# Moving the staging of the down-projection weights to the GpSimd queue and one group later, in an eight-core attention and FFN layer

## The chip, the cores and the metric

The kernel runs as one program on all 8 cores of a Trainium2 chip, with no traffic between the cores. The metric is the device time of the slowest core in microseconds. Each core handles half the tokens of one of four batch items, and holds its own copy of every weight.

## The reference

Everything is float32 with shapes x (4, 2048, 2048), 16 heads of 128, and an FFN width of 8192:

```python
def reference(x, w_atten, w_proj, w_gate, w_up, w_down):
    xn = layernorm(x)                                   # over the last axis, no affine
    q, k, v = split(xn @ w_atten.T)                     # 16 heads of 128
    q, k = rope(q), rope(k)
    att = softmax(causal(q @ k.T / sqrt(128)))
    s = (att @ v) @ w_proj.T
    h = silu(xn @ w_gate) * (xn @ w_up)
    h = keep_2_largest_of_4(h)                          # by magnitude, along the width
    g = silu(h @ w_down)
    return x + s * g
```

## The kernel before

A small recorder (`emit`, `dma`) notes for each of five engines a list of instructions, each with its waits on semaphores; `finalize` plays each list back in the order in which it was recorded. So an engine executes strictly in program order, and an instruction that waits holds back everything recorded behind it on the same engine. SP and POOL (GpSimd) issue the DMAs, each its own in that order. All buffers come from one SBUF arena that is reused by stages.

The stages on each core:

1. *Layernorm* (0 to about 185 us): x of all 2048 tokens of the batch item is loaded, normalized and kept in SBUF as bf16 (`xn`). `xn_done` are its four last instructions.
2. *Attention* (185 to 2115 us): a loop over 8 groups of two heads. For each group, the weights wk, wv and wq (2 MB of f32 each) are loaded by SP into the staging buffer `wstag2` and cast to bf16 by VectorE (L348). Then TensorE computes the K and Q units (12 of 16 matmuls each, L368); ScalarE evicts each unit (L381), a swap matmul (L390) and three VectorE operations (L393, L396, L404) apply RoPE. Two PSUM banks and two bf16 buffers rotate through the units, and the RoPE of a unit is recorded behind the matmuls of the next. V follows (L422), then scores, exp and PV for four pairs of head and query block (L457 to L492), each ended by a reciprocal (L504), a product on VectorE (L513) and a store of y from POOL. The weight casts wait for the last use of the bf16 weights by the group before.
3. *Out-projection* (from 2118 us): y is loaded back, w_proj is loaded and cast, `s` is stored to DRAM.
4. *Gate and up projections* (2325 to 3500 us) with the 2-of-4 selection, the result stored transposed as `d_hT`.
5. *Down-projection* (from 3505 us), which reads bf16 weights from the DRAM tensor `d_wdb`.

`d_wdb` is filled during stage 2: w_down (`wd`, 64 MB of f32) is loaded in pieces, cast by VectorE (L332) and spilled to `d_wdb` (32 MB of bf16) by POOL. Before the change this happens at the head of each group, ahead of that group's wk, wv and wq: 8 pieces of 1 MB for each of the 8 groups, in rows of 512 B (128 columns of f32), issued by SP into two f32 buffers and cast into two bf16 buffers. The load of piece s waits for the cast of piece s-2, and the cast of piece s for the spill of piece s-2. The loads of y and w_proj that open stage 3 wait for the last two spills.

`wstag2` has one buffer, so each of the three weight loads of a group waits for the cast of the one before it:

```python
            sl = 0
            t_l = kb.dma("sync", wstag2[sl][:].rearrange("p (c d) -> p c d", d=256),
                         srcw, sem,
                         [stag_free.get(sl)] + (xn_done if g == 0 else []))
            t_c = E("vector", lambda e, wbf=wbf, sl=sl: e.tensor_copy(
                wbf[:], wstag2[sl][:]), [t_l, wfree[nm]], "DVE")
            stag_free[sl] = t_c
```

Of the kernel before, what the change touches and what calls it, by code (L numbers as in the profile page):

```python
# [9 lines left out]
BF16 = mybir.dt.bfloat16  # L10
# [4 lines left out]
NF = C // 128  # L15
NT = T // 512
OWN = T // 2
NG = 8
# [96 lines left out]
def build_nc():  # L115
# [8 lines left out]
    wd = nc.dram_tensor("wd", [I, C], F32, kind="ExternalInput").ap()  # L124
# [10 lines left out]
    d_wdb = nc.dram_tensor("d_wdb", [128, NIC * C], BF16).ap()  # L135
# [11 lines left out]
    A = Arena(arena_t.ap(), ARENA_COLS)  # L147
# [18 lines left out]
    kb = KB(nc)  # L166
    E = kb.emit
# [38 lines left out]
    xn_done = []  # L206
# [75 lines left out]
        dbg_xn_tok = kb.dma("gpsimd", dbg["xn"][:], xn[:], "dbg0", xn_done)  # L282

    A.mark()
    wstag2 = [A.alloc(NF * 256)]
    wq_bf = A.alloc(NF * 128, BF16)
    wk_bf = A.alloc(NF * 128, BF16)
    wv_bf = A.alloc(NF * 128, BF16)
# [8 lines left out]
    recip = A.alloc(512)  # L297
    rep_sb = A.alloc(512)
    y_sb = A.alloc(256, BF16)
    wdp_st2 = [A.alloc(16 * 128) for _ in range(2)]  # L300
    wdp_bf2 = [A.alloc(16 * 64, BF16) for _ in range(2)]

    wqv = wq_bf[:].rearrange("p (c d) -> p c d", d=256)
    wkv = wk_bf[:].rearrange("p (c d) -> p c d", d=256)
# [14 lines left out]

    wdp_cast = {}  # L320
    wdp_spill = {}
    for g in range(NG):
        for j in range(8):
            s_ = g * 8 + j
            fcw, qi = s_ // 4, s_ % 4
            sl2 = s_ % 2
            srcw = wd[qi * 2048:(qi + 1) * 2048, fcw * 128:(fcw + 1) * 128]\
                .rearrange("(c p) d -> p c d", p=128)
            t_wpl = kb.dma("sync", wdp_st2[sl2][:].rearrange("p (c d) -> p c d", d=128),
                           srcw, "dWQ0" if sl2 == 0 else "dWQ1",  # L330
                           [wdp_cast.get(s_ - 2)] + (xn_done if s_ == 0 else []))
            t_wpc = E("vector", lambda e, sl2=sl2: e.tensor_copy(  # L332
                wdp_bf2[sl2][:], wdp_st2[sl2][:]),
                [t_wpl, wdp_spill.get(s_ - 2)], "DVE")
            wdp_cast[s_] = t_wpc
            t_wps = kb.dma("gpsimd", d_wdb[:, s_ * 2048:(s_ + 1) * 2048],
                           wdp_bf2[sl2][:], "dWDS0" if sl2 == 0 else "dWDS1", [t_wpc])
            wdp_spill[s_] = t_wps
        toks_w = {}
        for wi, (wap, wbf, nm, sem) in enumerate(  # L340
                ((wkT, wk_bf, "k", "dW0"), (wvT, wv_bf, "v", "dW1"),
                 (wqT, wq_bf, "q", "dW2"))):
            srcw = wap[:, g * 256:(g + 1) * 256].rearrange("(c p) d -> p c d", p=128)
            sl = 0
            t_l = kb.dma("sync", wstag2[sl][:].rearrange("p (c d) -> p c d", d=256),
                         srcw, sem,
                         [stag_free.get(sl)] + (xn_done if g == 0 else []))
# [3 lines that stand above are left out]
            toks_w[nm] = t_c  # L351
# [170 lines left out]
        kv_read_tok = group_pe_tail  # L522
        wfree = {"q": q_last_mm, "k": k_last_mm, "v": v_last_mm}

    ph2_tail_pe = kv_read_tok
    ph2_tail_dve = prev_y
    ph2_tail_act = prev_rpe
# [5 lines left out]
    wp_bf = [A.alloc(NF * 256, BF16) for _ in range(2)]  # L533
    s_stage = A.alloc(512)
    yav = y_all[:].rearrange("p (c x) -> p c x", x=OWN)
    wdp_last = [wdp_spill[62], wdp_spill[63]]
    t_yb = kb.dma("sync", yav, d_y[:, :].rearrange("(c p) x -> p c x", p=128), "dYB",
                  y_spills + wdp_last + [ph2_tail_pe, ph2_tail_dve, ph2_tail_act,
                                         stag_free.get(0), stag_free.get(1)])
# [392 lines left out]
```

How the kernel before makes its waits and increments, by code:

```python
                def body(handle):  # L76
                    for waits, fn, inc in ops:
                        for s, v in waits:
                            handle.wait_ge(sems[s], v)
                        ins = fn(handle)
                        if inc is not None:
                            s, by = inc
                            ins.then_inc(sems[s], by)
```

## Time and profile before

| | us |
|---|---|
| timed runs, median of 2 | 4029.93 |
| timed runs, lowest and highest | 4005.47, 4054.39 |
| the profiled execution, device time | 4059.74 |
| its span on the slowest core (core 6) | 4058.2 |
| spans of the eight cores | 3944.8 to 4058.2 |

| engine | busy us | share of the span |
|---|---|---|
| TensorE matmul (PE) | 2797.2 | 69% |
| TensorE weight load (PEld) | 1210.0 | 30% |
| VectorE (DVE) | 1329.8 | 33% |
| ScalarE (ACT) | 603.6 | 15% |
| GpSimd (POOL) | 226.5 | 6% |

The profile follows one execution on the slowest core. Busy time is the time in which an engine executes; DMA-issuing instructions are not counted as busy. Idle time is put down to the engine or transfer whose semaphore came last. "SPq" and "POOLq" are the queues that issue DMAs; a DMA's time to landing runs from its issue to the arrival of its semaphore. The granted clock of TensorE is given as a share of 2.4 GHz; 0.5 is the lower of its two levels. Buffer numbers are left out of the names, and as everything lies in one arena, most SBUF tiles read as `arena`.

### The profile page before, as it was taken

How to read it: one execution, taken by the hardware profiler on the slowest of the kernel's cores; microseconds unless marked ns; L12 is line 12 of the kernel's file. 1: busy time of each engine (PE TensorE's matmuls, PEld its weight loads, DVE VectorE, ACT ScalarE, POOL GpSimd, SP SyncE). 2: the span in 40 equal slices, each digit the busy share in tenths (PEclk: the TensorE clock that was granted, in tenths of full speed). 3: DMA queues.
4: the chain of work that ended last, by engine and by line, in shares of the span. 5: the costliest groups of instructions: out<-in, count | busy, mean ns of one | idle time of the engine just before them, and what ended most of it. 6: DMA issues, size and time to landing. Idle time of an engine off the chain costs nothing.

```text
span 4058.2 us, 34754 instructions; the slowest of 8 cores (3944.8 to 4058.2 us)
## 1 busy us (share of the span) xinstructions
PE 2797.2 (69%) x12377; PEld 1210.0 (30%) x12592; DVE 1329.8 (33%) x2087; ACT 603.6 (15%) x1102; POOL 226.5 (6%) x356
## 2 busy tenths in 40 slices
PE   2248385683838558383865769898889889399598
PEld 0013141321404123140411234343334334144244
DVE  4631131313213131221311046656657466300000
ACT  1102112030211203021120111111111111000000
POOL 0000000000000000000000100100001000011011
PEclk7668687886969778696887989999999999799799
DMA  4260512406041140604116176555465664455664
GB/s 150 84 171 3 149 42 67 124 4 188 3 137 53 53 139 4 188 2 121 49 34 207 69 158 156 122 142 135 104 146 131 135 141 99 144 177 210 198 209 155
DMA packets 513481, 466.99 MB, mean 115 GB/s; under 512 B 10144, under 2 KB 468896, under 8 KB 508832
## 3 DMA queue, kind: packets, MB, share of 16 engines
q1 hardware_dynamic: 486176, 376.65, 34.6%
q0 software_dynamic: 27136, 88.10, 6.5%
q8 instruction: 104, 1.70, 0.2%
q14 instruction: 65, 0.53, 0.0%
HBM read 393.41 MB, written 71.30 MB: 115 GB/s over the span
## 4 chain that ended last, share of the span: by engine, by line
PE 51%; DMA 23%; DVE 14%; issue 6%; SPq 3%; ACT 2%; DVEq 0%; ACTq 0%; POOLq 0%
PE ps L810 11%; PE ps L723 11%; PE ps L368 6%; PE ps L422 6%; DMA arena<-wd 5%; DMA d_hT<-arena 4%; DMA arena<-wkT 4%; PE ps L469 4%; PE ps L486 3%; SPq L66 3%; PE ps L457 3%; DVE arena L504 3%; PE ps L492 3%; PE ps L565 2%; DMA arena<-wqT 2%
## 5 line engine op out<-in xcount | busy, mean ns | idle before, releaser
L723 PE MATMUL ps<-arena 128*128 128x512 bf16 x4005 | 955.4, 394 | 34.1 <-DVE arena L699 27.6
L368 PE MATMUL ps<-arena 128*128 128x512 bf16 x1504 | 369.9, 400 | 472.8 <-DVE arena L348 468.6
L723 PEld LDWEIGHTS ps<-arena 128*128 128x128 bf16 x4096 | 412.2, 102 | 524.8 <-issue 90.6
L810 PE MATMUL ps<-arena 128*128 128x512 bf16 x2007 | 451.8, 384 | 95.8 <-issue 49.0
L368 PEld LDWEIGHTS ps<-arena 128*128 128x128 bf16 x1536 | 155.7, 102 | 683.9 <-issue 522.1
L504 DVE RECIPROCAL arena<-ps 1x512 f32<-1x512 f32 x32 | 107.1, 3346 | 757.2 <-PE ps L486 757.2
L810 PEld LDWEIGHTS ps<-arena 128*128 128x128 bf16 x2048 | 206.8, 101 | 340.5 <-issue 99.2
L473 ACT ACTIVATE arena<-ps 128x512 bf16<-128x512 f32 x384 | 229.3, 597 | 315.8 <-PE ps L469 306.4
L422 PE MATMUL ps<-arena 128*128 128x256 bf16 x2048 | 231.7, 274 | 0.0
L422 PEld LDWEIGHTS ps<-arena 128*128 128x128 bf16 x2048 | 203.4, 99 | 27.7
L735 DVE TENSOR_TENSOR arena<-arena,ps 128x256 f32<-128x256 f32 x256 | 105.3, 417 | 297.9 <-ACT arena L732 297.6
L699 DVE CAST arena<-arena 128x2048 bf16<-128x2048 f32 x128 | 157.2, 1228 | 135.9 <-DMA arena<-wgu 127.2
L732 ACT ACTIVATE arena<-ps 128x256 f32<-128x256 f32 x256 | 98.1, 384 | 690.4 <-PE ps L723 625.6
L469 PE MATMUL ps<-arena 128*128 128x512 bf16 x376 | 153.3, 408 | 64.1 <-PE ps L422 9.3
L381 ACT CAST arena<-ps 128x512 bf16<-128x512 f32 x96 | 56.3, 586 | 891.2 <-PE ps L368 751.1
L833 DVE TENSOR_TENSOR arena<-arena 128x512 f32<-128x512 f32 x32 | 22.2, 694 | 497.0 <-ACT arena L821 497.0
L565 PE MATMUL ps<-arena 128*128 128x512 bf16 x501 | 123.6, 398 | 87.6 <-ACT arena L572 47.5
L332 DVE CAST arena<-arena 128x2048 bf16<-128x2048 f32 x64 | 77.9, 1227 | 282.0 <-DMA arena<-wd 211.7
L457 PE MATMUL ps<-arena 128*128 128x512 bf16 x376 | 163.0, 433 | 6.8 <-PE ps L457 4.2
L664 PE MATMUL ps<-arena 128*128 128x128 bf16 x512 | 52.4, 228 | 157.3 <-DVE arena L647 154.3
L486 PE MATMUL ps<-arena 128*1 128x512 bf16 x384 | 152.9, 398 | 7.5 <-ACT arena L473 6.7
L66 POOL DMA_DIRECT2D d_hT<-arena x128 | 97.5, 762 | 1078.9 <-DVE arena L735 799.9
(71 smaller groups left out, 1841.6 us busy)
## 6 DMA issues: line engine op xcount, KB each, us to landing
arena<-wgu SPq DMA_DIRECT2D x128, 1024.0 KB, 15.5
arena<-wd SPq DMA_DIRECT2D x64, 1024.0 KB, 12.4
arena<-d_wdb SPq DMA_DIRECT2D x32, 2048.0 KB, 8.6
d_wdb<-arena POOLq DMA_DIRECT2D x64, 512.0 KB, 8.9
arena<-xT SPq DMA_DIRECT2D x4, 4096.0 KB, 16.1
arena<-wkT SPq DMA_DIRECT2D x8, 2048.0 KB, 20.6
arena<-wvT SPq DMA_DIRECT2D x8, 2048.0 KB, 8.3
arena<-wqT SPq DMA_DIRECT2D x8, 2048.0 KB, 9.4
```

The lines of the kernel that those rows point to most:

```text
L66: return self.emit(eng, lambda e: e.dma_start(out=out, in_=in_), waits, inc=sem, inc_by=16)
L368: tok = E("tensor", lambda e, f=f, h2=h2, bank=bank, tile=tile, wv_=wv_: e.matmul(ps[bank][:], wv_[:, f, h2 * 128:(h2 + 1) * 128], xnv[:, ...
L422: tok = E("tensor", lambda e, f=f, tc=tc, bank=bank: e.matmul(ps[bank][:, 0:256], xnv[:, f, tc * 128:(tc + 1) * 128], wvv[:, f, :], start= ...
L457: t_s = E("tensor", lambda e, qpos=qpos, h2=h2, a=a, sbank=sbank: e.matmul(ps[[0, 1, 4][sbank]][:], kh[:, h2 * T + qpos * 128:h2 * T + (qp ...
L469: t_mm = E("tensor", lambda e, mi=mi, sbank=sbank: e.matmul(ps[[0, 1, 4][sbank]][:], id_sb[:], mk_sb[:, mi * 512:(mi + 1) * 512], start=Fa ...
L473: t_e = E("scalar", lambda e, sbank=sbank, slot=slot: e.activation(pT[slot][:], ps[[0, 1, 4][sbank]][:], AF.Exp, bias=EXP_BIAS, scale=EXP_ ...
L486: last=(qi == nL - 1): e.matmul(ps[3][0:1, :], ones_colb[:, 0:1], pT[slot][:], start=first, stop=last),
L504: t_rcp = E("vector", lambda e: e.reciprocal(recip[0:1, :], ps[3][0:1, :]), [den_last, prev_rpe], "DVE")
L565: wpv=wpv: e.matmul(ps[bank][:], wpv[:, yc, cc * 128:(cc + 1) * 128], yav[:, yc, tt2 * 512:(tt2 + 1) * 512], start=(yc == 0), stop=(yc == ...
L699: t_gc = E("vector", lambda e, ip=ip, qt=qt, qs=qs: e.tensor_copy(wgu_bf[ip % 2][:].rearrange("p (c d) -> p c d", d=512) [:, :, qt * 128:( ...
L723: tok = E("tensor", lambda e, f=f, tc=tc, bank=bank, gv=gv: e.matmul(ps[bank][:], xnv[:, f, tc * 128:(tc + 1) * 128], gv[:, f, :], start=( ...
L810: tok = E("tensor", lambda e, ic=ic, bank=bank, wdv=wdv: e.matmul(ps[bank][:], wdv[:, ic, :], hTv[:, ic, :], start=(ic == 0), stop=(ic == ...
```

## The change

The staging of `wd` is put into a function `wdp_prep(g)`. It handles 16 pieces of 512 KB for a group instead of 8 of 1 MB, with one f32 and one bf16 buffer instead of two of each, and issues the loads from POOL instead of SP. The load of a piece waits for the cast of the piece before, and the cast for the spill of the piece before. It is recorded at the head of group g for group g-1, so group 0 begins without it, and once more after the last group for group 7. `wstag2` gets two buffers that alternate over the stream of weight loads. Stage 3 waits for the last two of the now 128 spills.

```diff
-    wstag2 = [A.alloc(NF * 256)]
+    wstag2 = [A.alloc(NF * 256) for _ in range(2)]
...
-    wdp_st2 = [A.alloc(16 * 128) for _ in range(2)]
-    wdp_bf2 = [A.alloc(16 * 64, BF16) for _ in range(2)]
+    wdp_st2 = [A.alloc(8 * 128)]
+    wdp_bf2 = [A.alloc(8 * 64, BF16)]
...
+    def wdp_prep(g):
+        for j in range(16):
+            s_ = g * 16 + j
+            fcw, qi = s_ // 8, s_ % 8
+            srcw = wd[qi * 1024:(qi + 1) * 1024, fcw * 128:(fcw + 1) * 128]\
+                .rearrange("(c p) d -> p c d", p=128)
+            t_wpl = kb.dma("gpsimd", wdp_st2[0][:].rearrange("p (c d) -> p c d", d=128),
+                           srcw, "dWQ0" if s_ % 2 == 0 else "dWQ1",
+                           [wdp_cast.get(s_ - 1)] + (xn_done if s_ == 0 else []))
+            t_wpc = E("vector", lambda e: e.tensor_copy(wdp_bf2[0][:], wdp_st2[0][:]),
+                      [t_wpl, wdp_spill.get(s_ - 1)], "DVE")
+            wdp_cast[s_] = t_wpc
+            t_wps = kb.dma("gpsimd", d_wdb[:, s_ * 1024:(s_ + 1) * 1024],
+                           wdp_bf2[0][:], "dWDS0" if s_ % 2 == 0 else "dWDS1", [t_wpc])
+            wdp_spill[s_] = t_wps
+
     for g in range(NG):
-        for j in range(8):
-            s_ = g * 8 + j
-            fcw, qi = s_ // 4, s_ % 4
-            sl2 = s_ % 2
-            srcw = wd[qi * 2048:(qi + 1) * 2048, fcw * 128:(fcw + 1) * 128]\
-                .rearrange("(c p) d -> p c d", p=128)
-            t_wpl = kb.dma("sync", wdp_st2[sl2][:].rearrange("p (c d) -> p c d", d=128),
-                           srcw, "dWQ0" if sl2 == 0 else "dWQ1",
-                           [wdp_cast.get(s_ - 2)] + (xn_done if s_ == 0 else []))
-            t_wpc = E("vector", lambda e, sl2=sl2: e.tensor_copy(
-                wdp_bf2[sl2][:], wdp_st2[sl2][:]),
-                [t_wpl, wdp_spill.get(s_ - 2)], "DVE")
-            wdp_cast[s_] = t_wpc
-            t_wps = kb.dma("gpsimd", d_wdb[:, s_ * 2048:(s_ + 1) * 2048],
-                           wdp_bf2[sl2][:], "dWDS0" if sl2 == 0 else "dWDS1", [t_wpc])
-            wdp_spill[s_] = t_wps
+        if g > 0:
+            wdp_prep(g - 1)
...
-            sl = 0
+            sl = (3 * g + wi) % 2
...
+    wdp_prep(NG - 1)
     ph2_tail_pe = kv_read_tok
...
-    wdp_last = [wdp_spill[62], wdp_spill[63]]
+    wdp_last = [wdp_spill[126], wdp_spill[127]]
```

## Rows read from the trace of the kernel before

**Rows 1.** Waits: engine line waited for: us in total, times, longest.
```profile
PE ps L368 <- DVE arena L348: 468.6, 8, 80.4
```

**Rows 2.** One stretch: PE, PEld, DVE, ACT, POOL busy, clock, DMA share, GB/s.
```profile
680.00:735.00 55.00, 0.00 (x0) 0.00 (x0) 12.16 (x10) 0.00 (x0) 5.19 (x9) 0.50 0.79 231
```

**Rows 3.** VectorE's timeline there: start us, us, instruction, idle before.
```profile
679.90 0.69 DVE L513 TENSOR_TENSOR arena<-ps,arena 128x512 bf16<-128x512 f32 x1 [3.16 <-ACT arena L510]
680.51 2.36 DVE L332 CAST arena<-arena 128x2048 bf16<-128x2048 f32 x2
...
724.90 1.23 DVE L332 CAST arena<-arena 128x2048 bf16<-128x2048 f32 x1 [4.71 <-DMA arena<-wd]
733.08 2.29 DVE L348 CAST arena<-arena 128x4096 bf16<-128x4096 f32 x1 [6.95 <-DMA arena<-wkT]
744.30 2.29 DVE L348 CAST arena<-arena 128x4096 bf16<-128x4096 f32 x1 [8.93 <-DMA arena<-wvT]
756.17 2.29 DVE L348 CAST arena<-arena 128x4096 bf16<-128x4096 f32 x1 [9.57 <-DMA arena<-wqT]
758.38 0.68 DVE L393 TENSOR_TENSOR arena<-arena 128x512 f32<-128x512 bf16 x1
```

**Rows 4.** Timeline of the SP queue, same stretch.
```profile
711.52 7.18 SPq L66 DMA_DIRECT2D arena<-wkT  x1
735.46 0.37 SPq L66 DMA_DIRECT2D arena<-wvT  x1
746.70 0.37 SPq L66 DMA_DIRECT2D arena<-wqT  x1
```

**Rows 5.** Timeline of ScalarE, same stretch: evictions of the K units.
```profile
741.63 0.59 ACT L381 CAST arena<-ps 128x512 bf16<-128x512 f32 x1 [61.97 <-PE ps L368]
745.09 0.59 ACT L381 CAST arena<-ps 128x512 bf16<-128x512 f32 x1 [2.87 <-PE ps L368]
759.15 0.59 ACT L381 CAST arena<-ps 128x512 bf16<-128x512 f32 x1 [13.48 <-DVE arena L393]
765.95 0.59 ACT L381 CAST arena<-ps 128x512 bf16<-128x512 f32 x1 [6.20 <-PE ps L368]
769.62 0.59 ACT L381 CAST arena<-ps 128x512 bf16<-128x512 f32 x1 [3.09 <-PE ps L368]
```

**Rows 6.** Timeline of POOL, same stretch.
```profile
681.13 0.72 POOL L66 DMA_DIRECT2D d_y<-arena  x1 [29.41 <-DVE arena L513]
682.27 0.73 POOL L66 DMA_DIRECT2D d_wdb<-arena  x1 [0.42 <-issue]
...
695.09 0.53 POOL L66 DMA_DIRECT2D d_wdb<-arena  x1 [11.14 <-DVE arena L332]
```

**Rows 7.** DMA issues: count, KB each, median us to landing.
```profile
arena<-wd SPq DMA_DIRECT2D x64, 1024.0 KB, 12.4
...
d_wdb<-arena POOLq DMA_DIRECT2D x64, 512.0 KB, 8.9
...
arena<-wvT SPq DMA_DIRECT2D x8, 2048.0 KB, 8.3
...
d_hT<-arena POOLq DMA_DIRECT2D x128, 128.0 KB, 3.1
...
d_s<-arena POOLq DMA_DIRECT2D x32, 256.0 KB, 2.6
...
d_y<-arena POOLq DMA_DIRECT2D x32, 128.0 KB, 2.0
```

**Rows 8.** The transfers of wd, whole span.
```profile
DMA to landing us min/median/max: 7.0/12.4/14.6
```

**Rows 9.** Group 0: SP's first wd issue, and ScalarE's eviction of K unit 3.
```profile
185.66 37.33 SPq L66 DMA_DIRECT2D arena<-wd  x8
...
281.49 0.59 ACT L381 CAST arena<-ps 128x512 bf16<-128x512 f32 x1 [5.97 <-PE ps L368]
```

**Rows 10.** SP's first issue of the out-projection stage.
```profile
2118.05 0.37 SPq L66 DMA_DIRECT2D arena<-d_y  x1
```

## The prediction, made before the result was known

> **What bounds the kernel now.** I read the page first. TensorE is busy for most of the span but idles in eight long holes, all in the attention stage between 185 and 2115 us. The table of waits puts 468.6 us of that idle time on one pair: the K matmuls of L368 wait for the weight cast of L348, eight times, 80.4 us at the longest [rows 1]. The question is what sits ahead of that weight cast, and for this I read one hole engine by engine, the one between groups 1 and 2.
>
> The stretch table shows the hole itself: from 680 to 735 us TensorE executes nothing, its clock is at the lower of its two levels (0.50 of 2.4 GHz), and the 16 DMA engines are 79% busy at 231 GB/s [rows 2]. VectorE's timeline shows why [rows 3]. The last attention output of the group (L513) ends at 680.59. Behind it in VectorE's program stand eight wd casts; they end at 726.13, most of them waiting for a load or a spill. Only then come the casts of wk (733.08), wv (744.30) and wq (756.17), each late by a transfer, because there is one staging buffer. RoPE starts at 758.38. SP's timeline gives the other side: wk is issued at 711.52, after the last wd load; wv at 735.46 and wq at 746.70, each behind the cast that frees the buffer [rows 4].
>
> What follows the hole is read from ScalarE's evictions [rows 5]. K unit 0 is evicted at 741.63, 6.3 us after the wk cast ends (735.37; the unit starts on the slow clock), unit 1 at 745.09, 3.46 us later. Then TensorE's swap matmul for the second RoPE waits for VectorE's first RoPE, which stands behind the wq cast, and unit 2's eviction waits 13.48 us. Unit 3 is evicted at 765.95; from there TensorE runs undisturbed. So one boundary costs 765.95 - 680.59 = 85.4 us, which I round to 85 and use for all seven boundaries between groups.
>
> **The change part by part.** Three things change: who issues the wd loads, how the wd work is cut and buffered, and how many staging buffers the QKV weights have.
>
> *VectorE's order does not change in kind.* The wd casts of group g-1 are now emitted at the head of group g, still ahead of the wk, wv and wq casts. VectorE executes in program order, so the weight casts still wait for the whole wd block, as in [rows 3]. The block of group 0 goes; a block after the last group comes. There remain eight blocks on the critical path, of 8 MB each.
>
> *The block becomes a serial chain.* It is now 16 steps with one f32 and one bf16 buffer. The load of step s+1 waits for cast s; cast s+1 waits for that load and for spill s. Nothing is loaded ahead, since the POOL queue holds the first load of a block behind the last y spill, and before two loads were always in flight or landed: the first two casts run back to back at 680.51. One step, s:
> - from VectorE's end to POOL's start 0.54 us (680.59 to 681.13). On POOL the spill stands ahead of the next load: 0.53 us to issue (695.09), then 0.42 us to the next instruction (681.13 + 0.72 to 682.27) [rows 6]. That is 1.5 us together.
> - the load from issue to landing, L.
> - 0.1 us to the cast (wq: issued 746.70, cast at 756.17 for a transfer of 9.4) and 0.7 us for the cast: 1.23 us for 2048 columns and 2.29 for 4096 [rows 3] make 0.16 + 0.52 per 1000, so 0.69 for 1024.
> - the spill, of 256 KB like POOL's stores of d_s (2.6 us, [rows 7]), is issued 0.95 us before the load and should land before it, so it adds nothing unless L is under about 2.
> So s = 2.3 + L.
>
> *L has no row.* No POOL load of 512 KB in 1024 runs of 512 B is in the trace. Four ways to bound it, from [rows 7]. Far below: POOL's 128 KB store of y lands in 2.0 us. Below: the quickest 1024 KB wd load from SP lands in 7.0 us [rows 8], and half of it is 3.5. Between: take 1.4 us fixed (2.0 less 128 KB at 231 GB/s) and the step's load and spill, 768 KB together, at the 231 GB/s of the hole, 3.4 us: 4.8. Above: 2.0 for y, 1.7 for 384 KB more at that rate, and a price for each run: d_hT (128 KB in 512 runs) takes 3.1 us against 2.0 for 128 runs, so 896 more runs add 2.6 us: 6.3. The last counts some of the cost of short runs twice. I take 5.0, near the middle value, and keep 3.5 to 6.3. Then s = 7.3 and a block is 117 us where 45.5 us stand now.
>
> The Trainium skill, DMA: Bandwidth & Descriptors, section on the anatomy of a SWDGE DMA, gives a fit of about 2.0 us plus bytes over 436 GB/s; for 512 KB that is an estimate of 3.2 us, so s of 5.5 and a change of +185 us instead of +415. The fit has no term for the length of the runs, while here d_hT and y, of the same bytes, differ by 1.1 us.
>
> *The QKV weights gain.* With SP free of wd and two staging buffers, wk and wv of the next group are loaded during the present one, hundreds of microseconds early. Call T0 the end of the block. The wk cast ends at T0 + 2.4, the wv cast follows at once, and wq is issued when the wk cast frees its buffer, lands 9.4 us later and is cast by about T0 + 14.3; RoPE starts then. By the spacing of [rows 5] (3.46, then 3.67 us) units 0 to 3 are evicted 6.3, 9.7, 13.4 and 17.1 us after the wk cast, and the swap matmul that stalled now finds its RoPE nearly done; I give it 0.3 us. Unit 3 is evicted at T0 + 19.9. Per boundary: 16 s + 20 - 85 = 16 s - 65.
>
> *Group 0.* Nothing stands ahead of wk now. It is issued at 185.66, where the first wd load is [rows 9]; alone a 2 MB load takes 8.3 us [rows 7], with wv behind it I give it 12. wk cast to 200.3, unit 3 evicted at 217.6 instead of 281.49: -64 us.
>
> *The end.* The last block, 16 s, stands wholly between the last y and the out-projection, since the loads of y and wp wait for the last two wd spills; SP issues the former at 2118.05 now [rows 10], about as long after the last y as it will be after the last spill: +16 s.
>
> *What costs nothing.* The same bytes are moved; stages 3 to 5 are untouched. The casts' busy time is about the same, 128 x 0.69 = 88 us against 64 x 1.23 = 79 us, already in s.
>
> **Sum:** 7 (16 s - 65) - 64 + 16 s = 128 s - 519 us. At s = 7.3: +415 us. The profiled execution took 4059.7 us, so 4475; it lies 30 us above the median of the two timed runs, 4029.9, and I forecast against the median: 4445 us. Within 2% (80 us) is what I call no change.
>
> **Rivals.**
> *A. The load lands fast.* L about 3.5, half the quickest wd load, because with one load in flight the DMA engines are unloaded. Then s = 5.8 and +223: 4253 us. For it: the DMA engines will be mostly idle. Against: half of a transfer's time also halves its fixed part. The rule of the skill named above lies here. Chance 0.22.
> *B. POOL's software queue is slow on 1024 short runs.* L = 7.9, between the quickest 1 MB load and the 8.9 us that POOL's 512 KB d_wdb spills take under load [rows 7]: s = 10.2, +787: 4817 us. For it: d_hT against y. Against: those medians come from crowded stretches. It decides from L above about 6.6. Chance 0.18.
> *C. It is not slower.* The weights' prefetch repays the serial chain. The break-even is s = 4.05, L = 1.8 us; up to s = 4.7, L = 2.4 us, the kernel is within 2%. That would need a 512 KB load to land like POOL's y store of 128 KB (2.0 us) or its d_s store of 256 KB (2.6 us); at 2.2 it gives +57: 4087 us. For it: nothing but the empty DMA engines. Chance 0.03.
> *Forecast*, L from 3.8 to 6.6: 0.57.
>
> **How the numbers follow.** The range runs from rival A's price, 4250, to L = 6.5, where 128 x 8.8 - 519 is +607: 4640. It leaves out most of B, C and the lower tail of A, 2 in 10. A, B and the forecast are all slower by over 2%; C holds 0.03 for the same, and I leave 0.01 for faster, an overlap that I do not see.
>
> **What the profile of the changed kernel will show.** Sixteen wd casts of 0.69 us ahead of each wk cast but the first, spaced 7.3 us apart and each waiting for its load; a TensorE hole of about 120 us before each of groups 1 to 7 and one of some 120 us between the last attention output and the out-projection; wk and wv casts back to back behind the block; unit 2's eviction no longer waiting 13 us for RoPE; the first K unit at about 200 us. The prediction is wrong if the spacing is off 7.3 us (each microsecond is 128 us of time), if the spill and not the load ends the wait of the casts, or if the loads of a block start before the last y.

## The result, and the profile after

| | before | after |
|---|---|---|
| median of the timed runs, us | 4053.72 (10 runs) | 4455.64 (13 runs) |
| lowest and highest, us | 4005.47, 4167.24 | 4383.4, 4588.76 |
| ratio after / before | | 1.089, 95% interval 1.083 to 1.095 |
| profiled execution, span of the slowest core, us | 4058.2 | 4422.6 |

The kernel became 8.9% slower. The ratio is made from runs in which no die was held at a lower clock than the other; the medians of the table are over all runs.

The stage borders, read from the SP queue's timeline, say where the time went. The kernel after, columns start us, us, instruction:

```profile
182.07 0.37 SPq L66 DMA_DIRECT2D arena<-wkT  x1
...
2506.86 0.37 SPq L66 DMA_DIRECT2D arena<-d_y  x1
```

Before, the last layernorm instruction ended and the first wd load was issued at 185.66 [rows 9], and the first transfer of the out-projection at 2118.05 [rows 10]: 1932 us of attention. After, 182.07 to 2506.86: 2325 us, so 392 us more. The rest of the span went from 1940 to 1916 us, 24 us less, and layernorm took 4 us less. The whole loss lies in the attention stage. (That is the slowest core of each execution. In the mean of the eight cores the first transfer of the out-projection starts at 2115 and at 2493 us, 378 us later, and the stages behind it are 30 us shorter.)

The waits of the whole span (waiting engine, line, what it waited for: us, times, longest):

```profile
PE ps L371 <- DVE arena L351: 843.1, 8, 116.0
DVE arena L332 <- DMA arena<-wd: 801.3, 128, 7.9
```

L371 is the old L368, L351 the old L348. TensorE's wait for the weight cast went from 468.6 us [rows 1] to 843.1, and every one of the 128 wd casts waits for its own load, never for a spill. VectorE at the boundary between groups 1 and 2:

```profile
663.32 0.69 DVE L516 TENSOR_TENSOR arena<-ps,arena 128x512 bf16<-128x512 f32 x1 [3.16 <-ACT arena L513]
670.02 0.70 DVE L332 CAST arena<-arena 128x1024 bf16<-128x1024 f32 x1 [6.02 <-DMA arena<-wd]
676.79 0.69 DVE L332 CAST arena<-arena 128x1024 bf16<-128x1024 f32 x1 [6.07 <-DMA arena<-wd]
...
774.13 0.69 DVE L332 CAST arena<-arena 128x1024 bf16<-128x1024 f32 x1 [7.41 <-DMA arena<-wd]
774.74 4.50 DVE L351 CAST arena<-arena 128x4096 bf16<-128x4096 f32 x2
788.94 2.29 DVE L351 CAST arena<-arena 128x4096 bf16<-128x4096 f32 x1 [9.70 <-DMA arena<-wqT]
791.15 0.69 DVE L396 TENSOR_TENSOR arena<-arena 128x512 f32<-128x512 bf16 x1
```

The output of the group ends at 664.01, where it ended at 680.59 before [rows 3]. Then the sixteen casts, 6.8 us apart for most, end at 774.82. The casts of wk and wv follow back to back; only wq still waits. POOL's timeline shows one step: cast end 670.72, spill issued at 671.26, next load at 671.80, its cast at 676.79.

```profile
671.26 0.55 POOL L66 DMA_DIRECT2D d_wdb<-arena  x1 [5.28 <-DVE arena L332]
671.80 0.91 POOL L66 DMA_DIRECT2D arena<-wd  x1
```

The DMA issue of the spills (count, KB each, median us to landing), and the landing of the wd loads (min/median/max):

```profile
d_wdb<-arena POOLq DMA_DIRECT2D x128, 256.0 KB, 2.3
```

```profile
DMA to landing us min/median/max: 4.6/4.9/6.3
```

The evictions after the hole, ScalarE, to be held against [rows 5]:

```profile
783.30 0.59 ACT L384 CAST arena<-ps 128x512 bf16<-128x512 f32 x1 [120.22 <-PE ps L371]
...
791.93 0.59 ACT L384 CAST arena<-ps 128x512 bf16<-128x512 f32 x1 [4.58 <-DVE arena L396]
796.57 0.59 ACT L384 CAST arena<-ps 128x512 bf16<-128x512 f32 x1 [4.05 <-PE ps L371]
```

Unit 2 (791.93) waits 4.58 us where it waited 13.48; unit 3 is evicted at 796.57.

### The profile page after: what moved, and what is told of

The parts are those of the page before. It is cut to its first block, busy times and chain, and to the rows that moved or that the text cites. A ratio compares the mean times of both kernels' runs of the same rounds, so it can differ in the third digit from the quotient of the medians.

```text
span 4422.6 us, 35311 instructions; the slowest of 8 cores (4308.5 to 4422.6 us)
## 1 busy us (share of the span) xinstructions
PE 2796.9 (63%) x12592; PEld 1203.5 (27%) x12592; DVE 1340.6 (30%) x2151; ACT 603.5 (14%) x1102; POOL 387.3 (9%) x548
## 4 chain that ended last, share of the span: by engine, by line
PE 46%; DMA 27%; DVE 13%; issue 7%; SPq 2%; ACT 2%; POOL 2%; DVEq 0%; ACTq 0%; POOLq 0%
DMA arena<-wd 14%; PE ps L814 10%; PE ps L727 9%; PE ps L371 6%; PE ps L425 5%; DMA d_hT<-arena 4%; PE ps L472 4%; PE ps L489 3%; PE ps L495 3%; PE ps L460 3%; SPq L66 2%; DVE arena L507 2%; DMA arena<-wgu 2%; DVE arena L332 2%; PE ps L569 2%
## 5 line engine op out<-in xcount | busy, mean ns | idle before, releaser
L727 PE MATMUL ps<-arena 128*128 128x512 bf16 x4096 | 952.1, 391 | 26.9 <-DVE arena L703 26.9
L371 PE MATMUL ps<-arena 128*128 128x512 bf16 x1536 | 363.4, 392 | 843.1 <-DVE arena L351 843.1
L814 PE MATMUL ps<-arena 128*128 128x512 bf16 x2048 | 454.4, 384 | 77.8 <-DMA arena<-d_wdb 77.8
L371 PEld LDWEIGHTS ps<-arena 128*128 128x128 bf16 x1536 | 152.1, 99 | 1046.3 <-issue 875.5
L332 DVE CAST arena<-arena 128x1024 bf16<-128x1024 f32 x128 | 88.9, 695 | 801.3 <-DMA arena<-wd 801.3
L569 PE MATMUL ps<-arena 128*128 128x512 bf16 x512 | 127.1, 405 | 200.6 <-DVE arena L557 151.6
L703 DVE CAST arena<-arena 128x2048 bf16<-128x2048 f32 x128 | 157.2, 1228 | 135.5 <-DMA d_s<-arena 84.8
L472 PE MATMUL ps<-arena 128*128 128x512 bf16 x384 | 159.5, 415 | 57.5 <-PE ps L460 0.4
L460 PE MATMUL ps<-arena 128*128 128x512 bf16 x384 | 168.3, 438 | 4.9 <-ACT arena L434 4.9
L495 PE MATMUL ps<-arena 128*128 128x512 bf16 x384 | 158.8, 414 | 0.0
## 6 DMA issues: line engine op xcount, KB each, us to landing
arena<-wqT SPq DMA_DIRECT2D x8, 2048.0 KB, 10.3
```

The lines of the kernel that those rows point to most:

```text
L371: tok = E("tensor", lambda e, f=f, h2=h2, bank=bank, tile=tile, wv_=wv_: e.matmul(ps[bank][:], wv_[:, f, h2 * 128:(h2 + 1) * 128], xnv[:, ...
L460: t_s = E("tensor", lambda e, qpos=qpos, h2=h2, a=a, sbank=sbank: e.matmul(ps[[0, 1, 4][sbank]][:], kh[:, h2 * T + qpos * 128:h2 * T + (qp ...
L472: t_mm = E("tensor", lambda e, mi=mi, sbank=sbank: e.matmul(ps[[0, 1, 4][sbank]][:], id_sb[:], mk_sb[:, mi * 512:(mi + 1) * 512], start=Fa ...
L495: first=(qi == 0), last=(qi == nL - 1): e.matmul(ps[2][:], vg[:, qpos * 256 + h2 * 128:qpos * 256 + (h2 + 1) * 128], pT[slot][:], start=fi ...
L569: wpv=wpv: e.matmul(ps[bank][:], wpv[:, yc, cc * 128:(cc + 1) * 128], yav[:, yc, tt2 * 512:(tt2 + 1) * 512], start=(yc == 0), stop=(yc == ...
L727: tok = E("tensor", lambda e, f=f, tc=tc, bank=bank, gv=gv: e.matmul(ps[bank][:], xnv[:, f, tc * 128:(tc + 1) * 128], gv[:, f, :], start=( ...
```

## The experiments

The first theory, that of the prediction: eight blocks of wd work lie on the path because VectorE meets them ahead of the weight casts, and a block is long because its pieces form a serial chain. The prediction gave two reasons for the chain, the single buffer and the spill that stands ahead of the next load on POOL; theory 1 below puts it on the second, POOL's program order. Rivals: the single buffer alone, POOL's queue alone, and a part of the block that lies beside other work. The size of the pieces and the delay by one group were not varied by themselves. All ran on all 8 cores; the kernel "before" was timed beside each.

### Two buffers, in the same order

```diff
-    wdp_st2 = [A.alloc(8 * 128)]
-    wdp_bf2 = [A.alloc(8 * 64, BF16)]
+    wdp_st2 = [A.alloc(8 * 128) for _ in range(2)]
+    wdp_bf2 = [A.alloc(8 * 64, BF16) for _ in range(2)]
...
-                           [wdp_cast.get(s_ - 1)] + ...
+                           [wdp_cast.get(s_ - 2)] + ...
...
-                      [t_wpl, wdp_spill.get(s_ - 1)], "DVE")
+                      [t_wpl, wdp_spill.get(s_ - 2)], "DVE")
```

> The changed kernel with two f32 and two bf16 buffers for wd (load s waits for cast s-2, cast s for spill s-2), all else as it is. Theory 1 (POOL's program order makes the chain): the load of piece s+1 is recorded behind the spill of piece s, which waits for cast s, so it is still issued only after that cast; the casts stay about 6.8 us apart and the time stays at the changed kernel's 4456 us, give or take 30. Theory 2 (the single buffer makes the chain): two loads are in flight, the casts come 3.5 to 4 us apart, and 128 x 3 us are gained: about 4070 us.

Measured: ratio to before 1.094 (1.092 to 1.097), whose interval meets that of the changed kernel (1.083 to 1.095). The casts waited 807.9 us for their loads, 801.3 in the changed kernel; with 0.69 us for each cast that is 7.0 us a step. The second buffer bought nothing: the instruction that would have filled it stands on POOL behind a spill that waits for the cast. The next kernel moves that instruction and nothing else.

### Two buffers, the load recorded ahead of the spill

```diff
         wdp_cast[s_] = t_wpc
+        if s_ % 16 != 15:
+            wdp_load(s_ + 1)          # waits for cast s_-1
         wdp_spill[s_] = kb.dma("gpsimd", ..., [t_wpc])
```

> As e1, but on POOL the load of piece s+1 is recorded ahead of the spill of piece s, so that two loads are in flight inside a block. Theory 1: now the chain loosens, to half of (1.5 + 4.9 + 0.8), or to what 768 KB take at the 231 GB/s of the old hole, 3.4 us; casts about 3.7 us apart, 128 x 3.1 us less than the changed kernel: about 4060 us. Theory 2 expects the same as it does of e1. If the 1024 short runs are bound in POOL's descriptor work, the casts stay above 5 us apart: over 4220 us.

Measured: ratio 0.996 (0.990 to 1.003). VectorE and POOL in a block:

```profile
655.45 0.69 DVE L338 CAST arena<-arena 128x1024 bf16<-128x1024 f32 x1 [2.64 <-DMA arena<-wd]
659.18 0.69 DVE L338 CAST arena<-arena 128x1024 bf16<-128x1024 f32 x1 [3.04 <-DMA arena<-wd]
662.63 0.69 DVE L338 CAST arena<-arena 128x1024 bf16<-128x1024 f32 x1 [2.75 <-DMA arena<-wd]
```

```profile
653.37 0.57 POOL L66 DMA_DIRECT2D d_wdb<-arena  x1 [2.19 <-DVE arena L338]
653.93 0.89 POOL L66 DMA_DIRECT2D arena<-wd  x1
```

The casts of a block come 3.6 us apart in the median where 3.7 were expected, and the whole loss of the change is gone. With two buffers, one line moved on POOL is worth a tenth of the time (1.094 to 0.996); the buffer without it is worth nothing. This kernel keeps the pieces of 512 KB, the delay by one group and POOL's queue; together with the gain of the staging buffers they come out even. POOL's descriptor work does not bound the loads at this pace. Theory 1 stands. The single-buffer rival is right in so far as with one buffer load s+1 waits for cast s wherever it is recorded.

### The wd loads from ScalarE's queue

```diff
-            t_wpl = kb.dma("gpsimd", wdp_st2[0][:]...
+            t_wpl = kb.dma("scalar", wdp_st2[0][:]...
```

> The changed kernel with the wd loads issued by ScalarE's queue in place of POOL's; buffers, sizes, waits and spills as they are. Theory 1: the load no longer stands behind the spill's issue on POOL (0.55 us) and is issued by a hardware queue as SP's were (0.37 us against 0.90), landing in 3.5 to 4.5 us; a step of about 5.2 us in place of 6.8, so 128 x 1.6 us less: about 4250 us, which still leaves the block serial and the kernel slower than before. Rival (the move to POOL is the whole loss): the time comes back to about 4054 us.

Measured: ratio 1.067 (1.061 to 1.073), median 4312 us. The rival is out: with the loads off POOL's queue a quarter of the loss is gone, not the whole. But the gain was 1.067 against 1.089, some 90 us, where I expected 200. Its waits, the timeline of VectorE and of the two queues, and the DMA issues show why.

```profile
DVE arena L332 <- DMA d_wdb<-arena: 662.2, 120, 8.1
```

```profile
665.52 0.69 DVE L332 CAST arena<-arena 128x1024 bf16<-128x1024 f32 x1 [6.12 <-DMA d_wdb<-arena]
671.52 0.69 DVE L332 CAST arena<-arena 128x1024 bf16<-128x1024 f32 x1 [5.31 <-DMA d_wdb<-arena]
```

```profile
666.29 0.37 ACTq L66 DMA_DIRECT2D arena<-wd  x1
666.74 0.54 POOL L66 DMA_DIRECT2D d_wdb<-arena  x1 [6.27 <-DVE arena L332]
```

```profile
arena<-wd ACTq DMA_DIRECT2D x128, 512.0 KB, 4.6
...
d_wdb<-arena POOLq DMA_DIRECT2D x128, 256.0 KB, 4.8
```

The load itself landed in 4.6 us, just above the 3.5 to 4.5 that I had guessed. But 120 of the 128 casts now waited for the spill, which landed in 4.8 us, where it took 2.3 in the changed kernel. The step is 6.0 us, set by a wait that the changed kernel does not have. Two things differ for the spill: the load is on another queue, and it goes out first. The cast ends at 666.21, ScalarE's queue issues the load 0.08 us later, and POOL issues the spill 0.45 us behind the load; in the changed kernel the spill goes 0.54 us ahead of the load.

### Loads and spills from ScalarE's queue

```diff
-            t_wps = kb.dma("gpsimd", d_wdb[:, ...
+            t_wps = kb.dma("scalar", d_wdb[:, ...
```

> As e3, with the spills too issued by ScalarE's queue, so that spill s stands ahead of load s+1 in one queue again. In e3 the casts were 6.0 us apart and 120 of 128 waited for the spill, which landed in 4.8 us in place of 2.3. Theory (a spill from POOL that runs beside a load of another queue is held up by it): with both in one queue the spill lands in some 2.5 to 3 us, the casts wait for the load again, and come 5.5 to 5.8 us apart: about 4250 us. Rival (the spill is slow because the DMA engines are loaded, whatever the queue): the spill still ends the casts' wait, 6 us apart, 4290 us.

Measured: 4269.9 us in one run, against 4024 to 4079 us in comparable runs of before beside it; no interval. Its waits and the DMA issue of the spills:

```profile
DVE arena L332 <- DMA arena<-wd: 637.4, 128, 7.6
```

```profile
d_wdb<-arena ACTq DMA_DIRECT2D x128, 256.0 KB, 2.3
```

The spill is back at 2.3 us, the load lands in 4.3, and all 128 casts wait for the load; by the waits (637.4 us) and the casts (88.9 us busy) the step is 5.7 us. The expectation put the spill's 4.8 us down to the other queue. This run does not show that, for with both in one queue the spill is also ahead of the load again, by 0.36 us. The trace of the kernel with the pieces spread and two buffers, further below, tells the two apart. At the head of a stretch it has two spills on POOL with a load between them, all on one queue:

```profile
616.01 0.54 POOL L66 DMA_DIRECT2D d_wdb<-arena  x1 [56.22 <-DVE arena L338]
616.54 0.91 POOL L66 DMA_DIRECT2D arena<-wd  x1
617.44 0.55 POOL L66 DMA_DIRECT2D d_wdb<-arena  x1
```

The first spill lands in 2.3 us, the second in 5.1:

```profile
DMA to landing us min/median/max: 5.1/5.1/5.1
```

The spill behind the load is late though no other queue is involved (another spill went out 1.4 us ahead of it too). All 36 spills of that core which follow a load by about 0.9 us land in 4.9 to 5.9 us. So a load that went out just before is enough to make a spill late, and the other queue is not needed for it. When the load moved to ScalarE's queue, it no longer waited for the spill's issue and went first. What in the DMA engines does that, the runs don't tell.

### No wd loads and casts

```diff
+    wdp_zero = E("vector", lambda e: e.memset(wdp_bf2[0][:], 0.0), xn_done, "DVE")
...
-            t_wpl = kb.dma("gpsimd", wdp_st2[0]...
-            t_wpc = E("vector", lambda e: e.tensor_copy(...
-            t_wps = kb.dma("gpsimd", d_wdb[:, ...], wdp_bf2[0][:], ..., [t_wpc])
+            wdp_spill[s_] = kb.dma("gpsimd", d_wdb[:, ...], wdp_bf2[0][:], ..., [wdp_zero])
```

> The changed kernel without the loads and casts of wd: its bf16 copy in DRAM is filled with zeros from one buffer, by the same 128 stores from POOL, none of which waits for VectorE. It leaves the down-projection's weights out, so that its time shows what the eight blocks cost. Theory 1: all eight blocks lie on the path, 128 steps of 6.85 us: 877 us less than the changed kernel, about 3580 us, with TensorE's holes at the group boundaries gone. Rival (a part of the blocks lies beside other work): less than 700 us is gained, over 3750 us. If the busier TensorE gets a lower granted clock in the later stages, these are a little longer than in the changed kernel.

Measured: 3592 us, ratio 0.887 (0.883 to 0.892); expected 3580. The eight blocks of the changed kernel, from the last product of a group to the last wd cast, sum to 890 us; (1.089 - 0.887) of about 4050 us is 818 us, 6.4 us for each of 128 steps. So all eight lie on the path, nearly in full. The sixteen stores of each block are still sent here, beside the weight loads of a group and, the last of them, ahead of the out-projection, so the full price is somewhat higher. The side guess that a busier TensorE pays with a lower clock in the later stages fell: from the load of y to the end this kernel took 1884 us against 1916. Its first transfer of the out-projection, SP's timeline:

```profile
1694.12 0.37 SPq L66 DMA_DIRECT2D arena<-d_y  x1
```

### One staging buffer again

```diff
-    wstag2 = [A.alloc(NF * 256) for _ in range(2)]
+    wstag2 = [A.alloc(NF * 256)]
...
-            sl = (3 * g + wi) % 2
+            sl = 0
```

> The changed kernel with one staging buffer for wk, wv and wq, as before the change. Only wk of the next group can be loaded ahead; wv is then loaded behind wk's cast and wq behind wv's. Theory 1: RoPE starts one transfer and one cast later at each of the eight groups, some 9 to 11 us each, less what the stalled units would hide: about +75 us, 4530 us. Rival (SP's freedom alone brings the gain, the second buffer nothing): 4456 us.

Measured: 4572 us in the profiled run, against 4424 in that of the changed kernel and a median of 4064 for before beside it; no interval. At one boundary, VectorE and ScalarE:

```profile
801.12 2.29 DVE L351 CAST arena<-arena 128x4096 bf16<-128x4096 f32 x1
813.44 2.29 DVE L351 CAST arena<-arena 128x4096 bf16<-128x4096 f32 x1 [10.03 <-DMA arena<-wvT]
824.87 2.29 DVE L351 CAST arena<-arena 128x4096 bf16<-128x4096 f32 x1 [9.13 <-DMA arena<-wqT]
```

```profile
827.85 0.59 ACT L384 CAST arena<-ps 128x512 bf16<-128x512 f32 x1 [13.51 <-DVE arena L396]
834.93 0.59 ACT L384 CAST arena<-ps 128x512 bf16<-128x512 f32 x1 [6.50 <-PE ps L371]
```

wv and wq are each late by a transfer again, and unit 2 waits 13.51 us as before the change [rows 5]. Unit 3 is evicted 33.7 us after the last wd cast (801.21) against 21.8 us in the changed kernel (774.82 to 796.57). In the mean of the seven boundaries it is 33.1 against 20.4 us, 12.7 us for each; the attention stage is 108 us longer. I expected 75, less than a transfer and a cast for each group, since I had let the stalled units hide a part. The direction holds, and SP's freedom alone is not the gain. The remaining 40 us of the 148 are in the later stages, which this kernel does not touch.

### The same pieces, spread over the group

One buffer, from POOL, with the changed kernel's waits; only the place of the pieces in the program moves.

```diff
-        if g > 0:
-            wdp_prep(g - 1)
+        if g == 0:
+            wdp_load(0)
...
         v_all = v_done[-1]
+        wdp_some(5)                    # cast, spill, load of the next piece
...
                 emit_denpv(nL - 1)
+                wdp_some(2 if a == 0 else (4 if h2 == 0 else 3))
                 t_rcp = E("vector", lambda e: e.reciprocal(...
```

> The changed kernel's 128 pieces with its one buffer, from POOL, with the same waits, but not recorded in one block: for each group 5 pieces behind the RoPE, 2 and 4 ahead of the reciprocals of the first head, 2 and 3 ahead of those of the second; the load of the next piece stands behind the spill of the last. Theory 1 (the place in VectorE's order is what costs, not the length of the chain): 16 x 6.85 = 110 us of chain fit beside the some 120 us of V and attention of a group; the blocks leave the path and about 877 us are gained against the changed kernel, less some tens of us where a cast delays a reciprocal: 3580 to 3680 us, faster than before. Rival (the chain itself costs wherever it stands, through delayed reciprocals): over 3900 us.

Measured: ratio 0.873 (0.871 to 0.876), 3533 us in the profiled run. VectorE in group 2, at the group's first reciprocal (L524), and the waits of VectorE and of TensorE:

```profile
663.17 0.69 DVE L338 CAST arena<-arena 128x1024 bf16<-128x1024 f32 x1 [6.08 <-DMA arena<-wd]
663.78 3.34 DVE L524 RECIPROCAL arena<-ps 1x512 f32<-1x512 f32 x1
```

```profile
DVE arena L338 <- DMA arena<-wd: 605.2, 96, 7.9
```

```profile
PE ps L527 <- DVE arena L524: 135.3, 32, 7.4
...
PE ps L386 <- DVE arena L366: 65.7, 8, 36.8
```

The step is as long as ever, 6.9 us, and VectorE still waits 605 us for the loads. But now it waits while TensorE works: TensorE's wait for the weight cast falls from 843 to 66 us. It is 12.7% faster than before. The place of the chain is the cause; its length is the price only where it stands on the path. It is even faster than the kernel without the wd loads and casts (0.887), which sends its sixteen stores beside the weight loads of each group: there the wq load lands in 16.1 us, here in 10.8. What is left of the chain's price is in the wait for the reciprocals, 135.3 us: in the kernel without the wd work, and in those with two buffers below, it is 105.2.

### The weight casts of the next group moved ahead as well

```diff
         rope_all = rope_done[-1]
+        if g + 1 < NG:
+            w_load(g + 1, "k"); w_load(g + 1, "v")
+            w_cast(g + 1, "k"); w_load(g + 1, "q")
...
         wdp_some(5)
+        if g + 1 < NG:
+            w_cast(g + 1, "v"); w_cast(g + 1, "q")
```

> As e6, and the casts of the next group's wk, wv and wq are recorded in the present group (wk behind its RoPE, wv and wq ahead of the first reciprocal), where the bf16 weights are free again. Theory 1: what is left of the boundary is the wait for the last reciprocal's chain and a slow start, and some 20 us of each of seven boundaries (wk cast, wq's load and cast ahead of RoPE) are gained over e6: about 3450 to 3550 us. Rival: the casts, which wait for wq's load, delay the first reciprocal by as much as they save at the boundary, and the time is that of e6.

Measured: ratio 0.896 (0.884 to 0.909): slower than the spread kernel. A miss, beyond even the rival, which expected the time of the spread kernel. TensorE's waits and VectorE's timeline, with the first reciprocal (L546):

```profile
PE ps L549 <- DVE arena L546: 247.8, 32, 25.3
```

```profile
449.78 0.69 DVE L338 CAST arena<-arena 128x1024 bf16<-128x1024 f32 x1
460.44 0.69 DVE L338 CAST arena<-arena 128x1024 bf16<-128x1024 f32 x1 [9.97 <-DMA arena<-wd]
...
484.23 0.69 DVE L338 CAST arena<-arena 128x1024 bf16<-128x1024 f32 x1 [9.13 <-DMA arena<-wd]
484.84 4.50 DVE L370 CAST arena<-arena 128x4096 bf16<-128x4096 f32 x2
498.00 0.70 DVE L338 CAST arena<-arena 128x1024 bf16<-128x1024 f32 x1 [8.66 <-DMA arena<-wd]
507.07 0.69 DVE L338 CAST arena<-arena 128x1024 bf16<-128x1024 f32 x1 [8.37 <-DMA arena<-wd]
507.68 3.34 DVE L546 RECIPROCAL arena<-ps 1x512 f32<-1x512 f32 x1
```

The wait for the weight cast is gone at the boundaries (36.0 us are left, all in group 0, of 65.7). But the first reciprocal of a group, at 507.68, stands behind seven pieces and two weight casts (484.84, 4.50 us), and the pieces are late. Beside the load of wq (issued at 449.94) one takes 10.7 us, not 6.9; beside those of wk (487.20) and wv (489.41) one takes 9.1, and one 13.8 with the two weight casts in it. A fourth took 9.8 us up to 484.23 with no weight load beside it, which stays open. TensorE waits 247.8 us for reciprocals, 135.3 in the spread kernel: 112 us lost for 30 gained. The attention stage ends 80 us later in the mean of the eight cores.

### Both mended

The casts of wv and wq move from ahead of the first reciprocal of a group to ahead of the second:

```diff
         wdp_some(5)
-        if g + 1 < NG:
-            w_cast(g + 1, "v"); w_cast(g + 1, "q")
...
                 emit_denpv(nL - 1)
+                if h2 == 0 and a == 1 and g + 1 < NG:
+                    w_cast(g + 1, "v"); w_cast(g + 1, "q")
                 wdp_some(2 if a == 0 else (4 if h2 == 0 else 3))
```

In the same kernel there are two wd buffers, with `wdp_load(s_ + 2)` behind the spill of piece s. A second kernel has these buffers and loads without the early weight casts, to tell the two apart.

> As e7, with two f32 and two bf16 buffers for wd, the load of piece s+2 recorded behind the spill of piece s, and the casts of the next wv and wq moved from ahead of the first reciprocal of a group to ahead of the second. In e7 TensorE waited up to 25.3 us for a group's first reciprocal, 247.8 us in all against 135.3 us in e6. Theory: that wait came from the pieces, each slowed from 6.9 to 9 or 10 us by the wv and wk transfers beside them, standing ahead of the reciprocal; with pieces some 3.5 us apart and the weight casts in a longer stretch the wait falls back to some 110 us, the boundary's 65.7 us of waiting for the weight cast goes, and the time is 60 to 90 us below e6's fast runs (3534 us): about 3460 us. Rival: the order on VectorE is so tight that any early cast delays a reciprocal by as much as it saves: 3530 us or more.

> As e6, with two buffers for wd and the load of piece s+2 recorded behind the spill of piece s; the weight casts stay at the head of the group. Theory: the chain of e6 already fits beside the work, but for some 4 to 7 us at the first reciprocal of a group; so at most 30 us are gained on e6's 3534 us: about 3510 us. Rival: the chain still costs in e6 and over 60 us are gained.

Measured: the one without early casts 0.865 (0.856 to 0.874), a median of 3509 us, some 30 us below the spread kernel's ratio, as expected. The one with them: 3460, 3508, 3515 and 3737 us, too far apart for an interval. The start of the out-projection, without early casts and with them, is sharper than the times:

```profile
1624.52 0.37 SPq L66 DMA_DIRECT2D arena<-d_y  x1
```

```profile
1570.27 0.37 SPq L66 DMA_DIRECT2D arena<-d_y  x1
```

TensorE's waits for reciprocals and weight casts without the early casts, then its wait for the weight casts with them (the reciprocals are at 105.2 us there too):

```profile
PE ps L528 <- DVE arena L525: 105.2, 32, 3.6
PE ps L387 <- DVE arena L367: 68.5, 8, 39.4
```

```profile
PE ps L399 <- DVE arena L370: 34.8, 1, 34.8
```

The wait for reciprocals is down from 135.3 to 105.2 us in both, so the second buffer does that: 30 us, and the out-projection starts 31 us earlier than in the spread kernel (1611 against 1643 us in the mean of the eight cores). The early casts take another 34 us off the wait for the weight casts, and the out-projection starts at 1576 us in the mean, 35 us earlier; the 54 us between the two rows above compare the latest core of one with an early core of the other. Together that is 66 us of the 60 to 90 that I expected in the time. How much of it reaches the end: on cores 0 to 3 the later stages took 1861 to 1878 us, as in the kernel without early casts (1861 to 1872), and their spans are 32 us shorter in the median (3447.5 against 3479.8). On cores 4 to 7 they took 1917 to 1936, and these set the time. Whether the late reciprocals of the kernel above were cured by the new place of the casts or by the buffers is not told apart: the early casts were not tried with one of the two edits alone.

## Why the prediction was right

I forecast 4445 us and measured 4456; the closeness of these two is partly luck. The median of before moved from 4030 to 4054 us with more runs, and the medians over all runs differ by 402 us, where the runs that the ratio is made from differ by 361. The change in time is the fairer test: +415 us forecast, +364 us in the spans of the two profiled executions, +361 us (0.089 of 4054) by the ratio. The sum was 50 us too large. Term by term, in the profiled executions:

| term | forecast | measured |
|---|---|---|
| L, load to landing | 5.0 us (3.5 to 6.3) | 4.9 us (4.6 to 6.3) |
| step s | 7.3 us | 6.8 us in the median, 6.95 mean |
| a block | 117 us | 111 us, mean of eight |
| last wd cast to unit 3 | 20 us | 20.4 us, mean of seven (18.8 to 22.5) |
| a boundary before the change | 85 us | 83.7 us, mean of seven |
| a boundary | +52 us | +48 us (131.5 against 83.7) |
| seven boundaries | +362 us | +335 us |
| group 0 | -64 us | -58 us |
| the end | +117 us | +113 us |
| inside the groups | 0 | +3 us |
| later stages and layernorm | 0 | -28 us |

So 23 us of the error lie in the attention stage, forecast at +415 and measured at +392, and 28 in stages that I had put at nothing.

*The order on VectorE, and eight blocks on the path.* Right, and shown: without the wd work the time is 3592 us, and with the same chain elsewhere 3533 in the profiled run.

*The serial chain.* Right that each piece waits for the one before. The prediction gave the single buffer as the first reason; the pair of two-buffer kernels shows that POOL's order holds the chain by itself: 1.094 with the old order, 0.996 with the load ahead. Neither alone would have shown it.

*The size of s.* The mean of 6.95 us is 0.35 us below the forecast, 44 us over 128 steps; smaller errors the other way (the tail of a boundary, the old boundary, group 0) took half of that back. By the prediction's own sign, a spacing off 7.3 us, this is its error. L was right; the middle of my four bounds served better than either end. The 0.42 us between two POOL instructions [rows 6] was counted twice. The first of the two wd casts at 680.51 [rows 3] took 1.23 us and ended at 681.74, and its spill started at 682.27: that is the 0.54 us from VectorE's end to POOL's start again, which the sum already had. In the changed kernel the load follows the spill's 0.55 us at once (671.26 to 671.80). Rival A gave +223 us; the estimate of 3.2 us from the Trainium skill's fit (DMA: Bandwidth & Descriptors, the anatomy of a SWDGE DMA) gave +185. The measured 4.6 us at the least speaks against both for this load on eight cores; whether the short runs or the other cores make the difference, no run tells. Rival B needed over 6.6 us and is out as well.

*The gains of staging.* Right in kind and, in the mean, in size. At the boundary shown, unit 3 came 19.5 us after the wk cast, where I had 17.4: wq landed in 10.3 us (median), not 9.4, and unit 2's eviction still waited 4.6 us. In group 0 the wk cast started 15.9 us after the issue of its load, with wv beside it (182.07 to 197.97), not 12.

*The later stages.* I had put them at nothing. They were 24 us shorter on the slowest core, 30 us in the mean of the eight (1901 to 1871 us). No instruction of theirs changed but what their first loads wait for. The cores of one execution differ by up to 99 us there (1841 to 1940 before, 1826 to 1916 after), and in the other kernels the mean of the eight runs from 1859 to 1908 us, without relation to how long TensorE idled earlier. I read it as scatter; it was not followed further.

## What to carry to other kernels

A transfer can be prefetched only as far as the queue that issues it lets it through: a second buffer is idle if its load is recorded behind an instruction that waits for the first. And before a chain of small waits is shortened, ask what it stands in front of; here the same chain cost over 800 us ahead of the weight casts and some 30 us between other work. When work is spread into a gap, count what it puts ahead of the next small instruction that another engine waits for, as the reciprocal here. And when a load is moved to another queue, look at which transfer now goes out first: the one behind may become the late one.

## What the runs showed of the hardware

- A 512 KB load in runs of 512 B from POOL lands in 4.9 us right behind a spill of 256 KB, 5.4 us with two loads in flight; from ScalarE's queue in 4.6 us ahead of POOL's spill and 4.3 us behind a spill of its own. Two in flight give a piece every 3.6 us, 768 KB in that time.
- A 256 KB spill lands in 2.3 us when it goes out ahead of a 512 KB load (by 0.54 us on POOL, by 0.36 us on ScalarE's queue), in 4.8 us when it follows a load of ScalarE's queue by 0.45 us, and in 5.2 us (median of 36) when it follows a load of its own queue by 0.9 us. Moving the load to ScalarE's queue (0.37 us to issue it against 0.90) put it first and made the store the late one.
- POOL takes 0.90 us to issue the load of 1024 runs, against 0.55 us for the spill of 128.
